# Two decoder layers on one core: an earlier first product, and the later weights of the self-attention stage loaded in pieces

## The reference, cut to what matters

```python
# layer 0, self-attention (the stage that is changed)
Q = (X @ Wq.T + bq).reshape(B, S, H, d_head) * scale
K = (X @ Wk.T + bk).reshape(B, S, H, d_head) * scale
V = (X @ Wv.T + bv).reshape(B, S, H, d_head)
scores = einsum('bqhd,bkhd->bhqk', Q, K)        # causal mask, softmax
out = einsum('bhqk,bkhd->bqhd', attn, V).reshape(B, S, D) @ Wo.T + bo
x = layernorm(x + out)
# weights that later stages use, prepared during this stage
w = quantise in blocks of 32 (w_gate), (w_up), (w_down)
```

## Time and profile before

| | |
|---|---|
| Runs without profiler | median 1120.88 us of 3 (1119.94 to 1123.54) |
| Profiled execution, its own time | 1128.16 us |
| Its span (first to last instruction) | 1126.2 us |
| Mean granted TensorE clock | 0.941 |
| First stage: start of item 1 / item 2 / item 8 / item 13 | 42.62 / 73.87 / 157.70 / 219.04 us |

### The profile page before, as it was taken

How to read it: one execution, slowest core, us unless ns; L and a number is a source line. 1 busy time by engine, 2 the same in 40 slices (tenths; PEclk the granted TensorE clock), 3 DMA queues, 4 the chain that set the end, 5 groups by cost and what they waited for, 6 DMA issues and landing times. The chain is left out here.

```text
span 1126.2 us, 25353 instructions
## 1 busy us (share of the span) xinstructions
PE 990.2 (88%) x8561; PEld 735.9 (65%) x8610; DVE 885.0 (79%) x2031; ACT 637.8 (57%) x1626; POOL 538.2 (48%) x983
## 2 busy tenths in 40 slices
PE   4669899983999966899999999999996999979996
PEld 3447667651555635788888888888884666546664
DVE  1448989933898967899999999999756899758885
ACT  2325555531798952555555555555452999944553
POOL 6337778873355543244444444444423465533322
PEclk8979999976899977999999999999998999989999
DMA  7888997733788530010000000003200666411111
GB/s 140 156 175 162 192 178 139 131 57 85 152 189 190 139 102 15 10 32 22 22 23 22 27 22 29 23 18 70 59 13 25 149 170 168 116 32 45 57 57 33
DMA packets 113631, 97.04 MB, mean 86 GB/s; under 512 B 16688, under 2 KB 106080, under 8 KB 113504
## 3 DMA queue, kind: packets, MB, share of 16 engines
q1 hardware_dynamic: 100032, 84.28, 33.7%
q10 hardware_dynamic: 11504, 8.98, 2.9%
q0 software_dynamic: 1968, 2.16, 1.2%
HBM read 64.97 MB, written 19.99 MB: 75 GB/s over the span
## 5 line engine op out<-in xcount | busy, mean ns | idle before, releaser
L402 DVE TENSOR_REDUCE ca_nm<-p_p 128x2 f32<-128x512 f32 x256 | 162.8, 678 | 19.0 <-PE p_p L300 17.7
L539 ACT ACTIVATE ca_pt<-p_p 128x512 f32<-128x512 f32 x256 | 142.7, 599 | 13.4 <-PE p_p L319 8.1
L300 PE MATMUL p_p<-ca_ks,ca_qs 96*128 96x256 bf16 x512 | 102.2, 284 | 19.6 <-DMA ca_ks<-k_parts 18.2
L1912 ACT ACTIVATE la_pq<-p_p,la_nm 128x128 f32<-128x128 f32 x256 | 90.1, 365 | 37.5 <-DVE la_nm L2015 37.5
L319 PE MATMUL p_p<-ca_qs,ca_ks 128*128 128x256 bf16 x512 | 101.4, 281 | 6.0 <-ACT ca_qs L531 2.4
L63 POOL TENSOR_TENSOR ca_pt<-la_lt,one 64x1024 f32<-64x1024 f32 x32 | 60.4, 1889 | 61.5 <-ACT la_lt L1891 60.3
L531 ACT ACTIVATE ca_qs<-p_p 32x1024 bf16<-32x1024 bf16 x64 | 65.0, 1016 | 43.0 <-PE p_p L309 41.5
L1896 ACT ACTIVATE la_qq<-p_p 128x512 f32<-128x512 f32 x32 | 19.1, 597 | 99.1 <-PE p_p L1728 99.1
L1066 DVE TENSOR_REDUCE sa_nm<-sa_p_s 128x4 f32<-128x512 f32 x64 | 43.7, 685 | 36.1 <-PE sa_p_s L926 35.6
L300 PEld LDWEIGHTS p_p<-ca_ks,ca_qs 96*128 96x128 bf16 x512 | 50.7, 101 | 32.5 <-DMA ca_ks<-k_parts 19.7
L1759 PE MATMUL p_p<-ca_pt,la_qq 128*128 128x128 f32 x512 | 70.4, 281 | 0.4 <-POOL ca_pt L63 0.3
(11 more groups left out here) (265 smaller groups left out, 2749.5 us busy)
## 6 DMA issues: line engine op xcount, KB each, us to landing
sa_qks<-sa_qkp SPq DMA_DIRECT2D x96, 128.0 KB, 5.0
ca_qs<-q_parts SPq DMA_DIRECT2D x32, 192.0 KB, 3.3
ca_ks<-k_parts SPq DMA_DIRECT2D x32, 192.0 KB, 3.8
ca_qs<-q_parts SPq DMA_DIRECT2D x32, 128.0 KB, 3.3
ca_ks<-k_parts SPq DMA_DIRECT2D x32, 128.0 KB, 3.8
ca_ct<-in_ctx_t SPq DMA_DIRECT2D x32, 128.0 KB, 3.7
ca_xr<-x_state SPq DMA_DIRECT2D x32, 128.0 KB, 2.1
x_state<-ca_xn SPq DMA_DIRECT2D x32, 128.0 KB, 2.1
```

What stands on the lines that cost most here:

```text
L300: last = pe.matmul(p_s[n % 3][:, qc, :], QS[b % 4][0:STACK, h, 128 * qc:128 * qc + 128], KS[b % 4][0:STACK, h, :], start=True, stop=True)
L402: dve.tensor_reduce(NM[b % 2][:, h, :], p_s[n % 3][:, :, :], AX.X, ALU.max, negate=True).then_inc(max_done, 1)
L539: act.activation(PT[g][:, j, :, :], p_e[n % 2][:, :, :], ACT.Exp, scale=SCALE).then_inc(exp_done, 1)
L1912: last = act.activation(PQ[g % 2][:, j, :], p_s[g % 2][:, j, :], ACT.Exp, bias=NM[b % 2][:, 4 * g + j:4 * g + j + 1], accum_out=SM[g % 2][ ...
```

## The change

The loads of the first stage are reordered, and some waits are split.

- Wq and Wk have a semaphore of their own, and TensorE's first product waits for those two. bq and bk, and Wv and bv, are issued from ScalarE's queue at its very start, with their own semaphores; `values(0)` and VectorE wait for Wv and bv.
- ScalarE runs a one-column activation (`early`) before its first bias.
- `raw[0]` is loaded from ScalarE's queue before item 0, not after it.
- `XT` has three buffers. SP loads `XT` of item 2 in its opening list, and `load_more(f)` loads `XT` of item f+3 where it loaded f+2.
- `load_weights` is called inside the step, after the exponentials of groups 1 and 3, and issues pieces: half of `AQN` at (item 0, group 1) and half at (0, 3), `AKT` at (1, 1), the first `AQR` and `ALN` at (1, 3), the four small ones at (2, 1), halves of `raw[1]` at (2, 3) and (3, 1), `AVT` at (3, 3), quarters of `AOW` in items 4 and 5, halves of `raw[2]` at (6, 1) and (6, 3), with `kv_ln` behind the last.

```diff
-IN_LOADS, OUT_LOADS = 8, 4
+IN_LOADS, OUT_LOADS = 9, 7
-        XT = [sb(f"xt{u}", [128, KC, S], F32) for u in range(2)]
+        XT = [sb(f"xt{u}", [128, KC, S], F32) for u in range(3)]
+        early = sb("early", [128, 1], F32)
             def load_more(f):
-                if f + 2 < B:
-                    sp.wait_ge(v_ready, f + 1)
-                    load_xt(f + 2)
+                if f + 3 < B:
+                    sp.wait_ge(v_ready, f + 1)
+                    load_xt(f + 3)
+                if f + 2 < B:
                     sp.wait_ge(c_rest, f + 1)
                     load_cx(f + 2)
             load_xt(0)
             for n in range(2):
-                sp.dma_start(W[n][:, :, :], ...).then_inc(qkv_loaded, 16)
-            for n in range(2):
-                sp.dma_start(BQK[n][:, :], biases_in[n]).then_inc(qkv_loaded, 16)
-            sp.dma_start(W[2][:, :, :], ...).then_inc(qkv_loaded, 16)
-            sp.dma_start(BV[:, :], bv_in.to_broadcast([128, D])).then_inc(qkv_loaded, 16)
+                sp.dma_start(W[n][:, :, :], ...).then_inc(qk_loaded, 16)
             load_xt(1)
             load_cx(0)
+            load_xt(2)
             load_cx(1)
                 if f == 0:
-                    pe.wait_ge(qkv_loaded, 16 * 6)
+                    pe.wait_ge(qk_loaded, 32)
             def values(f):
+                if f == 0:
+                    pe.wait_ge(v_loaded, 32)
                     if s == 0 and k == 0:
-                        dve.wait_ge(raw_loaded[n], 16)
+                        dve.wait_ge(raw_loaded[n], 16 if n == 0 else 32)
-            dve.wait_ge(qkv_loaded, 16 * 6)
+            dve.wait_ge(v_loaded, 32)
+            def load_weights(b, g):
+                if (b, g) == (0, 1):
+                    load_heads(AQN, q_b_nope_t, 0, 8, in_loaded)
+                if (b, g) == (0, 3):
+                    load_heads(AQN, q_b_nope_t, 8, 8, in_loaded)
+                if (b, g) == (1, 1):
+                    load_heads(AKT, kv_b_k_t, 0, 16, in_loaded)
+                if (b, g) == (1, 3):
+                    act.dma_start(AQR[:, 0], q_b_rope[0:128]).then_inc(in_loaded, 16)
+                    act.dma_start(ALN[:, 0:1], q_ln[0:128, :]).then_inc(in_loaded, 16)
+                if (b, g) == (2, 1):
+                    (ALN twice, AQR twice)
+                if (b, g) == (2, 3):
+                    load_raw(1, 0, 4)
+                if (b, g) == (3, 1):
+                    load_raw(1, 4, 4)
+                if (b, g) == (3, 3):
+                    load_heads(AVT, kv_b_v_t, 0, 16, out_w_loaded)
+                if b in (4, 5) and g % 2:
+                    (a quarter of AOW)
+                if (b, g) == (6, 1):
+                    load_raw(2, 0, 4)
+                if (b, g) == (6, 3):
+                    load_raw(2, 4, 4)
+                    (kv_ln twice)
-            act.wait_ge(qkv_loaded, 16 * 6)
+            for n in range(2):
+                act.dma_start(BQK[n][:, :], biases_in[n]).then_inc(bias_loaded, 16)
+            act.dma_start(W[2][:, :, :], ...).then_inc(v_loaded, 16)
+            act.dma_start(BV[:, :], bv_in.to_broadcast([128, D])).then_inc(v_loaded, 16)
+            act.wait_ge(const_set, 8)
+            act.activation(early[:, :], sh.one[:, :], ACT.Identity)
+            act.wait_ge(bias_loaded, 32)
+            load_raw(0, 0, 8)
                 for g in range(G):
                     exps(b, g)
+                    load_weights(b, g)
-                load_weights(b)
```

More of the change, by code:

```diff
@@ L702, in self_attention @@
         plain_stored, mask_loaded = sem("plain_stored"), sem("mask_loaded")
-        qkv_loaded = sem("qkv_loaded")
-        xt_loaded = [sem(f"xt_loaded{u}") for u in range(2)]
+        qk_loaded, bias_loaded, v_loaded = sem("qk_loaded"), sem("bias_loaded"), sem("v_loaded")
+        xt_loaded = [sem(f"xt_loaded{u}") for u in range(3)]
         cx_loaded = [sem(f"cx_loaded{u}") for u in range(2)]
@@ L768, in load_xt @@
             def load_xt(f):
-                sp.dma_start(XT[f % 2][:, :, :], x_t_in[f].rearrange("(c p) s -> p c s", p=128)).then_inc(xt_loaded[f % 2], 16)
+                sp.dma_start(XT[f % 3][:, :, :], x_t_in[f].rearrange("(c p) s -> p c s", p=128)).then_inc(xt_loaded[f % 3], 16)
             def load_cx(f):
@@ L873, in queries_keys @@
                             last = pe.matmul(p_x[:, D * n + 128 * o:D * n + 128 * o + 128], W[n][:, c, 128 * o:128 * o + 128],
-                                             XT[f % 2][:, c, :], start=(c == 0), stop=(c == KC - 1))
+                                             XT[f % 3][:, c, :], start=(c == 0), stop=(c == KC - 1))
                 last.then_inc(qk_ready, 1)
@@ L880, in values @@
                 wait(pe, v_biased, f)
+                if f == 0:
+                    pe.wait_ge(v_loaded, 32)
                 for c in range(KC):
-                    last = pe.matmul(p_v, XT[f % 2][:, c, :], W[2][:, c, :], start=(c == 0), stop=(c == KC - 1))
+                    last = pe.matmul(p_v, XT[f % 3][:, c, :], W[2][:, c, :], start=(c == 0), stop=(c == KC - 1))
                 last.then_inc(v_ready, 1)
@@ L1259, in context_middle, with load_raw @@
                 act.activation(CXP[f % 2][:, 1, :], CXR[:, :], ACT.Copy).then_inc(c_mid, 1)
-            def load_weights(b):
-                if b == 0:
-                    act.dma_start(raw[0][:, :].rearrange("p (t i) -> p t i", i=D),
-                                  mx_in[0].rearrange("(t p) i -> p t i", p=128)).then_inc(raw_loaded[0], 16)
-                if b == 1:
-                    act.dma_start(AQN[:, :, :], q_b_nope_t.rearrange("h p q -> p h q")).then_inc(in_loaded, 16)
-                    act.dma_start(AKT[:, :, :], kv_b_k_t.rearrange("h p l -> p h l")).then_inc(in_loaded, 16)
+            def load_raw(n, first, tiles):
+                width = INNER if n == 2 else D
+                at = slice(first * 2048 // 8, (first + tiles) * 2048 // 8)
+                rows = slice(first * 2048 // 8 // width * 128, (first + tiles) * 2048 // 8 // width * 128)
+                act.dma_start(raw[n][:, at].rearrange("p (t i) -> p t i", i=width),
+                              mx_in[n][rows].rearrange("(t p) i -> p t i", p=128)).then_inc(raw_loaded[n], 16)
@@ new lines, in load_heads @@
+            def load_heads(tile, source, first, heads, done):
+                at = slice(first, first + heads)
+                act.dma_start(tile[:, at, :], source[at].rearrange("h p q -> p h q")).then_inc(done, 16)
+            def load_weights(b, g):
[7 more added lines that the diff above has]
+                    act.dma_start(AQR[:, 0], q_b_rope[0:128]).then_inc(in_loaded, 16)
@@ L1278, in load_weights @@
-                if b == 4:
-                    act.dma_start(AVT[:, :, :], kv_b_v_t.rearrange("h p l -> p h l")).then_inc(out_w_loaded, 16)
+                if (b, g) == (2, 3):
[5 more added lines that the diff above has]
+                if b in (4, 5) and g % 2:
+                    quarter = 2 * (b - 4) + g // 2
+                    act.dma_start(AOW[:, 4 * quarter:4 * quarter + 4, :],
+                                  o_w[512 * quarter:512 * quarter + 512].rearrange("(h p) d -> p h d", p=128)).then_inc(out_w_loaded, 16)
@@ L1280, in load_weights @@
+                if (b, g) == (6, 1):
+                    load_raw(2, 0, 4)
+                if (b, g) == (6, 3):
+                    load_raw(2, 4, 4)
                     for n in range(2):
                         act.dma_start(sh.kv_ln[:, n, :], kv_ln.to_broadcast([128, 64])).then_inc(out_w_loaded, 16)
-                if b == 5:
-                    act.dma_start(AOW[:, :, :], o_w.rearrange("(h p) d -> p h d", p=128)).then_inc(out_w_loaded, 16)
-                if b == 7:
-                    act.dma_start(raw[2][:, :].rearrange("p (t i) -> p t i", i=INNER),
-                                  mx_in[2].rearrange("(t p) i -> p t i", p=128)).then_inc(raw_loaded[2], 16)
```

10 lines of the change are left out of this document (3 added, 7 removed).

## The result

| | before | after |
|---|---|---|
| Runs without profiler | median 1123.08 us of 11 (1119.94 to 1127.49) | median 1112.06 us of 11 (1105.94 to 1119.46) |
| Ratio after / before | | 0.990, 95% interval 0.9884 to 0.9925 |
| Profiled execution | 1128.16 us | 1109.13 us |
| Start of item 1 / 2 / 8 | 42.62 / 73.87 / 157.70 us | 46.95 / 61.09 / 145.76 us |

The change gains 11.0 us, 0.96% by the ratio. 21 us were forecast. The measured 1112.06 us lies just above the range of 1091 to 1111.

The account below looks back on a forecast made before the run. It took VectorE as the bound in items 8 to 12 and two serial stalls as item 1's loss. Gains of 2.0 us (opening) and 19.1 (items 1 to 7) took 1120.88 to 1099.8, say 1100 us; range 1091 to 1111.

Parts of the forecast that it names:

- (d): Opening up to item 1, with half of `AQN` added to DMA: item 1 starts at 40.6, a gain of 2.0 us.
- (h): Items 1 to 7 with weight pieces alongside: 13.95 us each for 1 to 6, 12.26 for 7; 19.1 us gained.
- (e): Opening: `raw[0]`, 3.6 us of DMA, fits 8.8 us free in the first 18; costed at nothing.
- (b): Opening: table load moves before the first bias; the chain feeding the stacks moves by 1.3 us, all issued at about 18.0.
- (c): Opening: item 2's product no longer stands before item 0's scores, which start at about 23 us, 5.2 us earlier.
- (a): Opening: TensorE's first product waits only for Wq and Wk and starts at 5.0 us, 2.0 us earlier.
- (f): Item 1: VectorE's wait of 8.0 us for `raw[0]` goes.
- (g): ScalarE's DMA issues, spread into groups of one to four: no old stall; costed at nothing, up to 0.5 us an item.
- (i): Check from DMA's side, 18 us to item 8: 123 us of work puts item 8's start between 126 and 139.
- (j): Item 8 and all later stages: unchanged, gain not given back; costed at nothing, with 2 us on either side.
- A: Rival, items 1 to 7: DMA becomes the bound, share staying at 0.96; gain 11.6, about 1109 us; chance 0.17.
- B: Rival, ScalarE's queue: it still stalls at `AKT` and `ALN`; gain 13, 1108 us; chance 0.08.

Follow-up runs that it names:

- run 9: The changed kernel itself, timed again unaltered beside later runs: 1112.66 us, ratio 0.992 to the kernel before.
- run 10: The changed kernel plus 28 unread TensorE products around the first scores of item 0: 1114.29 us, ratio 0.993 to the kernel before.
- experiment 3: The kernel before with only the new opening; later weights, `raw[0]` included, loaded as before: 1126.83 us, ratio 1.003.
- experiment 1: The changed kernel with `raw[0]` issued behind the first bias, about 6 us later: 1106.33 us, ratio 0.985 to the kernel before.
- experiment 2: The changed kernel with SP's mask stores issued ahead of `XT` of item 1, `raw[0]` left in place: 1108.45 us, ratio 0.987 to the kernel before.
- experiment 5: The changed kernel with `raw[0]` behind the first bias and mask stores ahead of `XT` of item 1: 1108.21 us, ratio 0.987 to the kernel before.
- experiment 6: As experiment 5, plus 28 unread TensorE products around the first scores of item 0: 1108.98 us, ratio 0.987 to the kernel before.
- experiment 8: As experiment 3, plus 28 unread TensorE products around the first scores of item 0: 1119.93 us, ratio 0.996 to the kernel before.
- experiment 11: As experiment 6, but pieces from item 2 on issued at the end of the step: 1109.44 us, ratio 0.989 to the kernel before.
- Experiment 4: The kernel before with only the weights in pieces inside the step and `raw[0]` behind the first bias; old opening: 1114.13 us, ratio 0.991.
- experiment 7: As experiment 5, but pieces issued at the end of the step instead of behind the exponentials: 1106.48 us, ratio 0.985 to the kernel before.
- Experiment 12: The changed kernel plus eight 0.5 MB DRAM-to-DRAM transfers on ScalarE's queue in items 2 to 6: 1114.28 us, ratio 0.994 to the kernel before.

## Why the prediction was wrong

The sum was 21.1 us: 2.0 in the opening and 19.1 in items 1 to 7. At item 8 the profile has 11.9: a loss of 4.3 in the opening and 16.3 (115.1 - 98.8) in items 1 to 7. Of the 9.2 us that are missing, 6.3 are missing at the start of item 1, where (d) had forecast 40.6, and 2.8 are (h)'s. The split holds for these two profiles; a later item 1 can make the items behind it shorter, as runs 9 and 10 show, so it is not a price of each part in the runs.

**The step that failed is (e)**, `raw[0]` costed at nothing in the opening. The cover named, 8.8 us of free DMA time in the first 18, exists, but most of it lies behind 10 us, while `raw[0]` was issued at 4.3. The prediction also looked for the harm in the wrong place: it feared for the stacks' own transfers, at up to 3.6 us. What suffered were two small stores that SP's in-order queue waits for before it can issue mask loads and then stacks: in the changed kernel they stood 7.6 us after the stores, without `raw[0]` (experiment 3) 5.1. Experiments 1 and 2 take that away in two ways and get 2.9 and 2.5 us back at item 1, and ratios of 0.985 and 0.987; by the medians of 1, 2 and 5 the runs gain 3.6 to 5.7 us of the 10.1 that were missing, though only experiment 1's interval lies apart from the changed kernel's. Step (b)'s "all issued at about 18.0" came true in both (18.16 and 18.13); in the changed kernel it was 20.90. Item 1 still came no earlier than 43.23 by this alone.

**(c) failed with it.** The product of item 2 was moved away from in front of the scores, and its 3.8 us were counted as saved. It did two things there: it cost time, and it had TensorE at work until the scores began. Without it TensorE stands for 6.6 us and scores run at the lower level. The prediction counted the product's 3.78 us as saved and priced everything behind it at the level of before. With TensorE kept at work, item 1 comes 2.8 us earlier (6 against 5), 2.0 (8 against 3) and 4.3 (10 against 9), but only 0.7 in experiment 11 against 5, where the opening is that of 6. Experiments 3 and 8 show it in the runs as well. The 40.46 of experiment 6, where 40.6 was forecast, is the best of these profiles. By these profiles (e) and (c) together are worth 4.4 us (experiment 11) to 6.5 us (experiment 6), against the 6.3 that are missing at item 1. With both mended the runs are at 1109 us, a gain of 12 to 14 us in place of 21: the rest of the miss isn't the opening's. In the profile of experiment 6, items 1 to 7 took 99.9 us where (h) has 96.0.

**(a), (b)** First product at 5.53 (forecast 5.0), first split at 12.96 (12.9), table load off the path: right in kind, but item 1 came later with them (experiment 3), and with the clock kept up only 0.5 us earlier (experiment 8).

**(f), (g)** Right: both stalls of item 1 are gone, 8.0 and 11.3 us. Experiment 4, which has no other part of the change, has the whole gain, and items 2 to 7 as a whole gave nothing. Pieces are issued in 0.35 to 0.78 us each in the profile after; in run 9 one took 1.41.

**(h)** 98.8 us where 96.0 was forecast, a term mis-sized by 3%. It was named as the likeliest to fail and was not the larger part. The mean was nearly right, the pattern not: items took 11.2 to 18.4 us and not 13.95 each. In item 3 the scores wait 3.4 us for stacks, and with the pieces moved by part of an item, item 3 takes 12.0 us and item 2 15.0 (experiment 7).

**(i)** The check failed: 126 to 139 was given, and item 8 started at 145.76. It left out `raw[2]`, which the change moves from behind item 7 to item 6, 3.6 us by its own price. And it treated the busy share as a fixed amount of work. In the changed kernel the share from 18 to 145.8 us sums to 133.5 us, above the 123 that were reckoned with and above 126.6 with `raw[2]`. Experiment 12 added 4 MB, 14.4 us at the 3.6 us a MB of the earlier trace rows, and the share of items 1 to 7 rose by 6 us only (109.5 from 103.5). The two stretches, 18 to 157.7 us before and 18 to 145.8 after, moved nearly the same bytes (23.40 and 23.62 MB) in as many packets, with 126.7 and 133.5 us of share: it can't be divided by a rate.

**(j)** Right: items 8 to 12 took 61.3 us, and nothing in what follows item 8 stands out of the scatter.

**The rivals.** A gave 1109 us and item 8 at 146, close to what was measured, but by a share that stays at 0.96 for 123 us of work; it was 1.04 for 133.5. Experiment 12 speaks against a bound on bytes: 4 MB more left items 3 to 6 within 0.6 us. A bound on packets stays untested. B and D didn't come; E and F neither. The Trainium skill (DMA: Bandwidth & Descriptors) advises to batch transfers to 1 MiB or more (section "Measured (HBM→SBUF, 128 partitions, SWDGE, issued from GpSimd)") and puts the fixed cost of one at about 2 us (section "Anatomy of one DMA — SWDGE (gpsimd) path", for transfers issued from GpSimd; the pieces here are issued from ScalarE). The estimate made from it, six pieces in series and 1112 us, hit the number by accident: six more pieces in items 0 to 6 left items 1 to 7 only 2.8 us above the forecast, and the larger part of the miss lies ahead of them.

**What stays open.** Experiments 1, 2, 5, 6 and 7 (0.985 to 0.987) lie below the changed kernel's 0.990 and 0.992, and aren't told apart from each other. How much of the gain is `raw[0]`'s early load and how much the pieces', and why item 1 starts near 44 us with the stores out of the way and TensorE not kept at work, beyond what the clock explains, wasn't run. Kept at work, TensorE gains 0.6% in the old arrangement of weights (8) and nothing measurable in the new (6, 10). In run 10 a longer wait for stacks stands behind it; in run 6 2.35 us are left at item 8, too few for these runs. Which stack loads and pieces must not meet was not worked out beyond experiment 7, and whether the number of packets bounds items 2 to 7 wasn't tested.

## What to carry to other kernels

A mean DMA share over the opening doesn't say that a transfer is free there: cut it at the moment of issue, and ask which small transfer beside it an in-order queue is waiting for. When work is moved from in front of the critical products, ask what keeps TensorE busy until they begin, since the clock may have been paid for by it. Run one kernel twice before reading a difference of 2 us from two profiles. And take a long stall out of a tuned kernel first: here the edit that removes the two stalls in item 1 gives the whole gain by itself, the new opening alone costs 0.3%, and parting two transfers in it gives 0.3 to 0.5% back.
